# Node stage of a graph network: attention dot products by four fused VectorE operations instead of a GpSimd product and a VectorE sum

## The reference, cut to what matters

```python
x = _layernorm(x + _L2_gnn_ref(x, edge_attr_128, src, dst, ...), axis=-1)
...
z2 = jnp.concatenate([h[src], h[dst], ex], axis=1)          # h = x, 128 + 128 + 2 columns
a = jax.nn.leaky_relu(z2 @ w_attn.T, negative_slope=0.01)[:, 0]
```

## Time and profile before

| | us |
|---|---|
| median of 3 runs | 3533.83 (3531.9 to 3536.51) |
| the profiled execution | 3541.67 |
| its span, to which all times below refer | 3539.8 |
| busy in the span: TensorE, VectorE, ScalarE, GpSimd | 2391.4, 2366.0, 2033.0, 2122.5 |
| loop of the node stage, first store of `x1` to last | 1280.1 to 1634.4 |
| first work of the next stage on ScalarE | 1709.06 |

### The profile page before, as it was taken

How to read it: one execution, slowest core, us unless ns; L and a number is a source line. 1 busy time by engine, 2 the same in 40 slices (tenths; PEclk the granted TensorE clock), 3 DMA queues, 4 the chain that set the end, 5 groups by cost and what they waited for, 6 DMA issues and landing times. The chain is left out here.

```text
span 3539.8 us, 54325 instructions
## 1 busy us (share of the span) xinstructions
PE 2391.4 (68%) x13252; PEld 1807.2 (51%) x13252; DVE 2366.0 (67%) x7373; ACT 2033.0 (57%) x6253; POOL 2122.5 (60%) x2026
## 2 busy tenths in 40 slices
PE   6757772599966776774577677666656657777430
PEld 4523331466645555553466566545446657776330
DVE  6669991244458869987466677699834459978442
ACT  5624441567731159997577777789834448875110
POOL 7737773277600048773677577577577767710776
PEclk9979996599978888887788788877778879987555
DMA  6735555577719954553577788789778689943231
GB/s 183 207 106 154 156 152 112 165 241 247 239 54 285 297 169 165 171 171 126 172 232 221 231 267 264 241 265 285 228 228 224 196 228 277 265 128 105 84 91 41
DMA packets 521816, 678.87 MB, mean 192 GB/s; under 512 B 98910, under 2 KB 285669, under 8 KB 521504
## 3 DMA queue, kind: packets, MB, share of 16 engines
q1 hardware_dynamic: 455202, 549.18, 50.0%
q0 software_dynamic: 65856, 125.82, 13.5%
q10 hardware_dynamic: 446, 0.40, 0.0%
HBM read 398.69 MB, written 280.39 MB: 192 GB/s over the span
## 5 line engine op out<-in xcount | busy, mean ns | idle before, releaser
L1495 POOL DMA_INDIRECT xg<-r_d,src_row x392 | 426.3, 1087 | 170.0 <-issue 115.5
L1495 POOL DMA_INDIRECT xg<-x_d,src_any x392 | 415.1, 1059 | 154.2 <-issue 116.7
L1829 POOL DMA_INDIRECT look<-table_d,ids x196 | 202.1, 1031 | 360.2 <-DVEq L1784 303.7
L2885 POOL DMA_INDIRECT out<-x_f,out_row x196 | 203.0, 1036 | 176.8 <-DVE x_f L2951 118.0
L1128 POOL DMA_INDIRECT xd<-in_x,ids x196 | 216.0, 1102 | 73.2 <-issue 51.1
L1495 POOL DMA_INDIRECT xg<-g_d,src_any x196 | 200.6, 1024 | 79.3 <-issue 52.1
L718 POOL DMA_INDIRECT rows_d<-row,slot_i x196 | 193.5, 987 | 69.5 <-issue 56.7
L2259 ACT ACTIVATE term_c<-xg,scale 128x128 f32<-128x128 f32 x392 | 125.3, 395 | 149.7 <-DMA xg<-r_d,src_row 71.4
L2611 ACT ACTIVATE term_c<-term_c,inv_deg 128x128 f32<-128x128 f32 x392 | 124.9, 392 | 130.8 <-DVE term_c L2627 130.7
L2225 PE MATMUL m_ps_c<-w_L_gnn_Wr,term_t_c 128*128 128x128 f32 x784 | 129.6, 317 | 104.2 <-ACT m_c L2250 104.2
L2171 DVE TENSOR_TENSOR_SCAN agg_t_c<-flags_c,agg_t_c,t_ps_c 128x512 f32<-128x512 bf16 x144 | 183.4, 1274 | 3.9 <-PE t_ps_c L2553 3.8
(11 more groups left out here) (510 smaller groups left out, 8407.4 us busy)
## 6 DMA issues: line engine op xcount, KB each, us to landing
flags_c<-cont_d SPq DMA_DIRECT2D x245, 128.0 KB
xm<-rows_d SPq DMA_DIRECT2D x49, 512.0 KB
m_d<-m_c SPq DMA_DIRECT2D x98, 256.0 KB, 4.4
r_d<-r_c SPq DMA_DIRECT2D x98, 256.0 KB
m_in_c<-m_d SPq DMA_DIRECT2D x98, 256.0 KB
x_c<-x_d SPq DMA_DIRECT2D x98, 256.0 KB, 4.3
e_c<-rows_d SPq DMA_DIRECT2D x98, 256.0 KB
g_d<-g_f SPq DMA_DIRECT2D x50, 258.0 KB
```

The source lines that it names most:

```text
L1495: pool.indirect_dma_start(out=xg[:, n % SC, k, 0:width], out_offset=None, in_=table, in_offset=bass.IndirectOffsetOnAxis(ap=rows[:, t:t + ...
L1829: pool.indirect_dma_start(out=look[:, t, :], out_offset=None, in_=table_d[:, :], in_offset=bass.IndirectOffsetOnAxis(ap=ids[:, 0, t:t + 1] ...
L2885: pool.indirect_dma_start(out=out[:, :], out_offset=bass.IndirectOffsetOnAxis(ap=out_row[:, t:t + 1], axis=0), in_=x4[:, n % SF, k, :], in ...
```

## The change

GpSimd's product and VectorE's sum over it become four operations on VectorE, one for each of a group's four rows per partition. Each multiplies `u` by `a0` and adds up the products in the same pass, and an accompanying read writes the sum to one column of `dotk`. They stand where the sum stood. GpSimd keeps its lookups and gathers and has no product; the semaphore `attended` and the waits on it go.

```diff
             def dense_dve(dve, it):
                     if g >= 3:
                         dve.wait_ge(normed.sem, normed.at(g - 2))
-                        dve.wait_ge(attended.sem, attended.at(g - 2))
...
                 g = it - 8
                 if 0 <= g < NG:
-                    dve.wait_ge(attended.sem, attended.at(g + 1))
-                    dve.tensor_reduce(dotk[:, g % 2, :], dotw[:, g % 2, :, :], AX.X, ALU.add).then_inc(attended_sum.sem, 1)
+                    for k in range(K):
+                        made = dve.tensor_tensor_reduce(out=dotw[:, g % 2, k, :], in0=u[:, g % 3, k, :], in1=a0[:, k, :], scale=1.0, scalar=0.0,
+                                                        op0=ALU.mult, op1=ALU.add, accum_out=dotk[:, g % 2, k:k + 1])
+                    made.then_inc(attended_sum.sem, 1)
...
             def dense_pool(pool, it):
-                g = it - 7
-                if 0 <= g < NG:
-                    pool.wait_ge(added_u.sem, added_u.at(g + 1))
-                    if g >= 2:
-                        pool.wait_ge(attended_sum.sem, attended_sum.at(g - 1))
-                    pool.tensor_tensor(dotw[:, g % 2, :, :], u[:, g % 3, :, :], a0[:, :, :], ALU.mult).then_inc(attended.sem, 1)
                 if 1 <= it <= LOOKS:
```

More of the change, by code:

```diff
@@ L1548, in graph_kernel @@
             summed_2, added_u = signal("summed_2"), signal("added_u")
-            attended, attended_sum = signal("attended"), signal("attended_sum")
+            attended_sum = signal("attended_sum")
             spread_ok, rooted_n, inv_ready, normed = signal("spread_ok"), signal("rooted_n"), signal("inv_ready"), signal("normed")
@@ L1903, in graph_kernel @@
             retire([(looked, TILES), (setup, 1), (rows_found, 1), (spread_ok, NG + 7), (rooted_n, NG + 7), (inv_ready, NG + 7), (normed, NG)])
-            retire([(s, NG) for s in (logit_ready, sloped_g, x1s_ready, x2s_ready, turned_g, g1o_ready, attended, attended_sum)])
+            retire([(s, NG) for s in (logit_ready, sloped_g, x1s_ready, x2s_ready, turned_g, g1o_ready, attended_sum)])
             retire([(x_in[s], len(range(s, NG, 6))) for s in range(6)] + [(x4_out[s], len(range(s, NG, 3))) for s in range(3)])
```

## The result

The changed kernel takes 3511.13 us (median of 5 runs, 3506.06 to 3519.11) against 3536.51 for the kernel before (5 runs, the three shown above among them), 25.4 us less. The ratio is 0.993 with an interval of 0.9912 to 0.9948, that is 18 to 31 us. So I compare stages inside the profiles.

The account below looks back on a forecast made before the run. ScalarE, closely followed by VectorE, was taken to bound the node stage's loop, and GpSimd's gathers its end. Terms -23.7 + 3.0 - 5.2 = -25.9 us took the median from 3533.83 to 3508, range 3500 to 3524.

Parts of the forecast that it names:

- The bound at the end: Node stage's end: GpSimd alone sets the time; without products its 28 gathers start earlier, -23.7 us (-26.7 to -22).
- the landing: Last `x1` stores before the gathers: taken to land in 4.4 us, plus 0.3 us of issue to the first gather.
- GpSimd's own ending: From GpSimd's last gather to the next block: 9.4 us, taken as GpSimd's ending cost that moves along with the gathers.
- The fused operations: VectorE in the loop: 285 ns plus an 83 ns read, overlapping; four take 0.82 us, path grows 0.23 us per group.
- The serial rival: Fused operations don't overlap on VectorE: four cost 1.47 us, loop +22.4 us, kernel 3527 us; chance 0.06.
- What they cost the loop: Loop: ordinary iterations absorb the longer VectorE path, late-TensorE and non-waiting ones pay; +3.0 us, bounds 0 and +9.0.
- The holds: Loop: products held VectorE in six slow iterations of 51.38 us; without them all become quiet, -5.2 us (bounds 0, -5.2).
- The waits: VectorE: its two waits on `attended` go and a new one on `attended_sum` comes, claimed to change nothing.
- The loop as a whole: Node stage's loop over 48 groups: all effects apart from the stage's end together, -2.2 us.
- Fused operations held by indirect DMAs: Loop: lookups beside the fused operations hold them, 1.4 us per group over 35 iterations, +49; kernel 3554 us; chance 0.05.
- An end that moves nothing: Stage's end hangs on something other than GpSimd, so only the loop's -2.2 us is left: 3532 us; chance 0.07.
- the prediction's own sign: Loop: the forecast is wrong in size if the rhythm of 7.69 us grows by more than 0.1.

Follow-up runs that it names:

- e2: Kernel before with GpSimd's product and VectorE's reduction kept for groups 0 to 41, fused operations for the last six; 3508.71 us, ratio 0.9934.
- e4: Changed kernel with each fused operation over columns 0 to 63 of 128 only, in the same place; node stage loop plus end 402.4 us, rhythm 7.65.
- e3: Changed kernel with the four fused operations and the two small operations on their results moved behind `y2`; 3494.51 us, ratio 0.9903.
- e8: The changed kernel itself measured once more, against the kernel before; 3509.0 us, ratio 0.9927.
- e1: Changed kernel, except that GpSimd waits for the last addition of `u` before the 28 gathers; 3533.25 us in one run.
- e5: Changed kernel, with GpSimd's old product also made for groups 0 to 41 into a tile nothing reads; 3497.18 us in a single run.

## Why the prediction was right, and where it was not

- **The bound at the end: right.** The forecast of -23.7 us came out as -25.9. The term that was a little off is the landing: from the issue of the last store to the first gather I had 4.7 us from a store in another stage, and measured 3.03; in all kernels without held gathers it lies between 2.97 and 3.03. The 28 gathers take 36.33 us against 36.17 and give back 0.2 us, where I had 0.7.
- **GpSimd's own ending: right.** From the end of the last gather to the next stage it is 9.38 to 9.40 us in every profile, whenever the gathers ran, so it moved along as assumed. What passes in it is not shown.
- **The fused operations: right in price.** 288 and 83 ns, and four of them hold VectorE for 0.84 us, so the path grew by 0.84 - 0.59 = 0.25 us where I had 0.23. The serial rival is not borne out: the read of the accumulator starts 0.20 us after a fused operation that lasts 0.28. (That rival's own sum took off the reduction's record of 676 ns and not its 0.59 us on the path; with these it would have come to 3530 instead of 3527.) In the Trainium skill, "VectorE: DVE Perf Modes", the section on the DRAIN says that the next operation does not start until the pipe is empty, but also that one that is not held starts earlier; I had used the first half alone, and the trace agrees with the second.
- **What they cost the loop: wrong in size.** I had 0.23 us in one of four iterations and nothing in the others, +3.0 us in all and +9.0 at most. Between the 17th and the 45th reciprocal alone, behind the slow iterations, the loop lost 222.8 - 214.3 = 8.5 us (7.5 against e2), 0.30 per iteration. The step that failed is "costs nothing" for an ordinary iteration. Every second iteration does stay at 7.30, but those between them grow: four iterations of the kernel before take 7.30, 7.47, 7.30 and 8.70 us, six of the change 7.30, 7.73, 7.30, 8.84, 7.30 and 9.31. e4 (shorter, same place) and e3 (same length, later place) both take the loss away, so it comes from what stands ahead of `y2`. The path from there, a later `y2`, a late TensorE that reaches ScalarE more often (13 waits for 7), is argued from the waits and not shown by itself: e2, with nearly the rhythm of the kernel before, has 10 of these waits between 1320 and 1600 us, against 6 before and 12 with the change.
- **The holds: right, by e4 nearly in size too.** The six iterations that took 51.38 us take 1368.16 - 1320.49 = 47.67 with the change: -3.7 instead of -5.2, because the new rhythm is longer by 0.30 in each than the quiet one I compared with. e4, in its one run, has no products and about the old path: there they take 45.6, -5.8. The reading that a product holds nothing elsewhere was not quite right: three more operations of the kernel before take 0.88 to 1.99 us between 1453 and 1472.
- **The waits: not nothing.** I had put the end of VectorE's waits on `attended` at nothing. In iteration 8 of the kernel before, the first with a product to sum up, the reduction waits for it:

```profile
1311.70 0.69 DVE L1738 TENSOR_REDUCE dotk_n<-dotw_n 128x4 f32<-128x512 f32 x1 [1.31 <-POOL dotw_n L1825]
```

That iteration takes 8.33 us, and 7.15 with the change. Up to the 11th reciprocal the kernel before takes 58.8 us and e2 59.2; the change, e8 and e1 take 55.5 to 56.8. How much of this is the wait and how much the filling of the pipeline, which varies between equal kernels, stays open.
- **The loop as a whole** came out at +1.9 us where I had -2.2 (+2.3 by the means of the loops that repeat): rounded, -3.3 up to the 11th reciprocal, -3.7 in the six iterations, +8.5 up to the 45th and +0.5 behind it.
- **The rivals.** Fused operations held by indirect DMAs: not seen, 350 ns at most. An end that moves nothing: the next stage's start moved with the gathers, in the change and back again in e1.

The sum, 25.9 us forecast and 25.4 measured between the medians, 24.0 in the stage's profile, is thus nearer than its parts: an end that gave 2 us more and a loop that cost 4 us more. That closeness is luck; e8's stage gained 21.3. By the prediction's own sign, a rhythm that grows by more than 0.1 us, the loop's size was wrong: it grew by 0.22, and the end paid for part of it.

Two things stay open: why the holds of e5 don't lengthen its loop, and what spreads equal loops by 3.4 us. The spread lies at the loop's two ends: against the change, e1 takes 3.2 us more up to the 12th reciprocal and 2.2 more behind the 45th.

## What to carry to other kernels

Look at what stands in front of an engine's last burst in its own queue: a small product that costs nothing all through a loop can hold back 28 transfers at its end, and moving the last six products did as much here as moving all 48. Where work goes to another engine, ask not only whether it fits but what of that engine's output others wait for, and put the new work behind that. And an order that is best with one set of neighbours needn't be so with another: by the rhythm, the sum belongs ahead of `y2` while GpSimd multiplies and behind it once it doesn't.

## What the runs showed of the hardware

After GpSimd's last indirect DMA the end of this block takes 9.38 to 9.40 us in all twelve profiles.

A VectorE operation with two inputs in the on-chip memory waits out a GpSimd product that it meets, also if it has only 4 columns (up to 1.99 us instead of 0.22 at line 1741 of the kernel before), while the product keeps its 1.26 to 1.30 us. One input is no sure way out: a `tensor_scalar` on 4 columns with one input, line 1781 of the kernel before, took 2.02 us beside a product instead of 0.17. A reduction with one input of 512 columns runs beside it at its usual 676 ns.

A hold can begin before the product does: that of line 1781 began at 1346.99, 0.70 us ahead of the product's record and beside the lookup in front of it; why is not shown. Where no product follows, the indirect DMAs, which keep GpSimd busy for 11.93 of 18 us, don't hold the fused operations: the longest of 192 takes 350 ns.
